# A graph layer with experts on one core: bucket ranks, counts and the last mixing moved to TensorE, slots spread out, short products put into waits

## The reference

```python
edge_index = jnp.stack([src, dst])                       # 100000 edges, 6250 nodes
xn = _layernorm(x)                                       # x: 6250 x 256
messages = xn[dst] * edge_weight[:, None]
agg = segment_sum(messages, src, 6250)
gin = relu((xn + agg) @ W1 + b1) @ W2 + b2               # 256 -> 512 -> 256
# mix: 8 heads; k, v = normed heads of xn; out = q (k^T v / N) + xn
x = x + gin + mix(xn)
y = _layernorm(x)
logits = y @ gate_w + gate_b                             # 16 experts, the best 2
h = relu(y @ w1[e] + b1[e]); o = h @ w2[e] + b2[e]       # 256 -> 512 -> 256
z = y + sum_k softmax(top2)[k] * o[k]
return x + layernorm(z) * gamma + beta
```

## Time and profile before

| what | value |
|---|---|
| median of 3 runs (lowest, highest) | 2381.49 us (2380.33, 2381.5) |
| profiled execution: its time, its span | 2381.34 us, 2379.1 us |
| block 1 | 0 to 501 us; counts ready at 92.5, sorting groups from 213 |
| block 2 | 501 to 1719.5 us; gathers issued 512.0 to 1687 |
| blocks 3 and 4 | 1719.5 to 2265.6 us; first expert tile's matmul 1753.69 |
| block 5 | 2265.6 to 2379.1 us |
| busy | PE 69%, DVE 61%, POOL 58%, ACT 31% |

### The profile page before, as it was taken

How to read it: one execution, slowest core, us unless ns; L and a number is a source line. 1 busy time by engine, 2 the same in 40 slices (tenths; PEclk the granted TensorE clock), 3 DMA queues, 4 the chain that set the end, 5 groups by cost and what they waited for, 6 DMA issues and landing times. The chain is left out here.

```text
span 2379.1 us, 40341 instructions
## 1 busy us (share of the span) xinstructions
PE 1638.3 (69%) x9284; PEld 1371.2 (58%) x9285; DVE 1453.1 (61%) x4177; ACT 739.9 (31%) x2173; POOL 1391.3 (58%) x1512
## 2 busy tenths in 40 slices
PE   5602788624556887787878777776569999999900
PEld 2202777613555776676766656654468888888800
DVE  8499988637676666666665665654343443434379
ACT  4803789500000344322222222221213333333200
POOL 8001788748876776677777777776225554555400
PEclk9856899856778999898898889888679999999955
DMA  4000011254333444344444444447581111111184
GB/s 153 0 0 16 20 35 34 20 104 134 115 113 89 133 127 120 108 128 120 127 121 125 124 119 125 124 118 98 77 288 57 62 62 57 60 61 61 52 290 149
DMA packets 133498, 233.44 MB, mean 98 GB/s; under 512 B 28775, under 2 KB 85199, under 8 KB 133374
## 3 DMA queue, kind: packets, MB, share of 16 engines
q0 software_dynamic: 56384, 145.17, 22.8%
q1 hardware_dynamic: 49294, 61.00, 8.4%
q10 hardware_dynamic: 27696, 25.83, 3.4%
HBM read 189.48 MB, written 42.43 MB: 97 GB/s over the span
## 5 line engine op out<-in xcount | busy, mean ns | idle before, releaser
L1278 POOL DMA_INDIRECT lower<-xn_rows,lower x864 | 865.0, 1001 | 310.5 <-issue 239.3
L1303 PE MATMUL bank<-lower 128*128 x960 | 342.9, 443 | 145.4 <-SPq L1154 121.3
L1439 DVE TENSOR_TENSOR xh<-xh,bank 128x256 f32 x480 | 199.7, 416 | 285.9 <-PE bank L1304 285.1
L1422 DVE TENSOR_SCALAR lower<-iota_n,lower 128x128 f32<-128x128 f32 x960 | 294.4, 357 | 69.7 <-issue 56.2
L606 POOL DMA_INDIRECT edge_records_sorted<-lower x112 | 200.8, 1793 | 205.1 <-ACT lower L717 174.9
L1304 PE MATMUL bank<-lower 128*128 x960 | 320.5, 419 | 0.0
L1303 PEld LDWEIGHTS bank<-lower 128*128 128x128 f32 x960 | 177.7, 213 | 212.1 <-issue 200.0
L650 PE MATMUL bank<-lower 128*64 128x128 f32 x1568 | 189.8, 285 | 125.1 <-ACT lower L701 120.8
L650 PEld LDWEIGHTS bank<-lower 128*64 128x64 f32 x1568 | 183.6, 145 | 128.8 <-DVE lower L915 121.4
L1834 POOL DMA_INDIRECT expert_rows<-arena,dest_idx x114 | 114.6, 1005 | 213.7 <-DVE arena L1929 196.5
L1920 DVE TENSOR_SCALAR arena<-bank,b_tile 128x128 f32<-128x128 f32 x456 | 128.4, 344 | 178.4 <-PE bank L1863 178.4
(11 more groups left out here) (316 smaller groups left out, 2530.4 us busy)
## 6 DMA issues: line engine op xcount, KB each, us to landing
lower<-xn_rows,lower POOLq DMA_INDIRECT x864
lower<-in_L_ffn_w SPq DMA_DIRECT2D x16, 512.0 KB, 9.7
upper<-in_L_ffn_w SPq DMA_DIRECT2D x16, 512.0 KB, 10.5
xn_rows<-xh SPq DMA_DIRECT2D x7, 896.0 KB, 4.1
arena<-xn_rows ACTq DMA_DIRECT2D x7, 896.0 KB, 5.5
lower<-xn_rows ACTq DMA_DIRECT2D x49, 128.0 KB
xn_rows<-lower ACTq DMA_DIRECT2D x49, 128.0 KB
x_plus_beta<-lower ACTq DMA_DIRECT2D x49, 128.0 KB
```

Source lines behind the costliest of these rows:

```text
L1278: pool.indirect_dma_start(edge_rows[:, t % ROUND, :], None, xn_dram, bass.IndirectOffsetOnAxis(source.bitcast(U32)[:, t:t + 1], 0)).then_i ...
L1303: pe.matmul(sums_at(u), edge_sel[:, 2 * u % ESEL, :], rows_flat[:, ds(at, D)], start=True, stop=False)
L1422: dve.tensor_scalar(edge_sel[:, (2 * u + h) % ESEL, :], iota_n[:], lane[:, at:at + 1], weight_s[:, at:at + 1], ALU.is_equal, ALU.mult).the ...
L1439: dve.tensor_tensor(xh[:, at], xh[:, at], sums_at(u), ALU.add).then_inc(s_acc, 1)
```

## The change

- **Counts and ranks.** Buckets are also stored place by place (`bkt_c`: for each of the 28 places the 28 groups side by side). Differences for a distance d are now two matmuls with the identity and its negative (`ident_b`, `minus_b`) into two banks, ScalarE squares from there and compares in bf16, and TensorE adds the result into banks 6 and 7 with the identity; GpSimd has no part. After every fourth distance TensorE does one counting round. Masks follow `bkt_c`, so a counting matmul reads runs of 28 neighbours. The two restart masks come from GpSimd, beside. The loop over buckets is written out and takes starts directly.
- **Fewer tiles.** ET is rounded up to 2 instead of 24: 858 tiles and 429 pairs (864 and 432 before); 480 units as before. The zeroed area stays at 864.
- **Order in block 2.** Slots are spread by 15/2 units instead of 14/3; `head_sums` eight units after a group's start; head rows are normed in place in two buffers, the next group loaded earlier; `stage_h` two units ahead; `mark` later, the last one in block 3.
- **Short products** (`spin`): ident x before, 128 columns fp32, into an unused part of bank 7: 38 in the last slot and its ranks, 18 at block 3, 25 at block 4.
- **Weights.** Block 3 loads only expert 0; experts 1 to 3 follow after the second row load of block 4 has landed. gamma is loaded in block 3.
- **Last mix.** ScalarE puts the mixing weights on diagonals, TensorE adds xh and both expert rows in a bank, VectorE reads mean, variance and values from it. The first and last groups are small (1, 1, 2, 3 and 3, 2, 1, 1 tiles), four row loads are in flight instead of three.

```diff
-    ET = -(-(NGRP * ((GC * P + NT * (QE - 1)) // QE)) // (TQ * ROUND)) * ROUND
+    ET = -(-(NGRP * ((GC * P + NT * (QE - 1)) // QE)) // (2 * TQ)) * 2
+    ZT = -(-ET // 8) * 8
@@ block 1, TensorE
+                def differences(d):
+                    if d > 2:
+                        pe.wait_ge(s_gapsq, d - 2)
+                    for h, lo, hi in halves_from(d):
+                        to = bank[2 + 2 * (d % 2) + h][:, 0:hi - lo]
+                        pe.matmul(to, ident_b, bkt_c[:, lo:hi], start=True, stop=False)
+                        mm = pe.matmul(to, minus_b, bkt_c[:, lo - d * NGRP:hi - d * NGRP], start=False, stop=True)
+                    mm.then_inc(s_gap, 1)
+                def add_same(d):
+                    pe.wait_ge(s_same, d)
+                    for h, lo, hi in halves_from(d):
+                        mm = pe.matmul(bank[6 + h][:, lo - h * EH:hi - h * EH], ident_b, same[d % 2][:, lo:hi],
+                                       start=False, stop=hi - lo == NGRP)
+                    mm.then_inc(s_local, 1)
-                    matched = match[p].rearrange("p (b g j) -> p b g j", g=NGRP, j=GC)
+                    matched = match[p].rearrange("p (b j g) -> p b j g", g=NGRP, j=GC)
-                        mm = pe.matmul(bank[p][:, 0:GT * NGRP], upto_b, matched[:, :, :, c], start=c == 0, stop=c == GC - 1)
+                        mm = pe.matmul(bank[p][:, 0:GT * NGRP], upto_b, matched[:, :, c, :], start=c == 0, stop=c == GC - 1)
+                for d in range(1, GC):
+                    add_same(d)
+                    if d + 2 < GC:
+                        differences(d + 2)
+                    if d % 4 == 3:
+                        count(d // 4)
@@ block 2
-        turn_unit = [max(slots_from + 1 + -(-14 * s // 3), done_by[s + 1] + 2) for s in range(NT)]
+        turn_unit = [max(slots_from + 1 + -(-15 * s // 2), done_by[s + 1] + 2) for s in range(NT)]
+        def spin(pe, n):
+            for _ in range(n):
+                pe.matmul(bank[7][:, D:D + P], ident[:], before[:], start=True, stop=True)
-                            if u == heads_from[g] + 4 + k // 2:
+                            if u == heads_from[g] + 8 + k // 2:
                                 head_sums(g, k)
+                        if u == rank_unit[-1]:
+                            spin(pe, 10)
+                    for f, later, spins in ((gate, T_GATE, 2), (turn_xn2, T_TURN2, 14), (second, T_SECOND, 6), (hidden, T_HIDDEN, 3),
+                                            (turn, 0, 3)):
@@ block 4, SP
+                    if e == 0:
+                        sp.wait_ge(s_tok[1], 16)
+                        for later in range(1, WAHEAD):
+                            load_weights(sp, later)
@@ block 5, TensorE
+                        if t >= FBANK:
+                            pe.wait_ge(s_fcen, t - FBANK + 1)
+                        pe.matmul(mixed, ident[:], xh[:, t * D:(t + 1) * D], start=True, stop=False)
+                        pe.wait_ge(s_fdiag, TOPK * (t + 1))
+                        pe.matmul(mixed, diag[t % NDG * TOPK], first_row(t), start=False, stop=False)
+                        pe.matmul(mixed, diag[t % NDG * TOPK + 1], second_row(t), start=False, stop=True).then_inc(s_fmix, 1)
@@ block 5, VectorE
-                        dve.scalar_tensor_tensor(first[k], first[k], weight(k, 0), xh[:, (t0 + k) * D:(t0 + k + 1) * D],
-                                                 ALU.mult, ALU.add).then_inc(s_dve, 1)
-                        dve.scalar_tensor_tensor(first[k], second[k], weight(k, 1),
-                                                 first[k], ALU.mult, ALU.add).then_inc(s_fmix, 1)
-                        dve.bn_stats(stats[:, k0 + k, :], first[k]).then_inc(s_dve, 1)
+                        dve.bn_stats(stats[:, k0 + k, :], bank[(t0 + k) % FBANK][:, 0:D]).then_inc(s_dve, 1)
```

More of the change, by code:

```diff
@@ L178, in gps_layer @@
         last_row = early(P)
-        apart = [early(EC) for _ in range(3)]
+        bkt_c = early(EC // 2).bitcast(BF16)
+        ident_b, minus_b = (early(P // 2).bitcast(BF16) for _ in range(2))
+        apart = [early(EC // 2).bitcast(BF16) for _ in range(2)]
+        same = [early(EC // 2).bitcast(BF16) for _ in range(2)]
         early = carver(row_hot[1], GC * P)
-        rank = early(EC)
-        same = [early(EC) for _ in range(3)]
+        restart_g, restart_b = (early(NT * NGRP) for _ in range(2))
         row_hot = [a.rearrange("p (j r) -> p j r", j=GC) for a in row_hot]
@@ L581, in _ @@
                                    pattern=[[0, P]], channel_multiplier=1).then_inc(s_consts, 1)
[L585 to L597, removed]
+                for a, first in ((restart_g, bg(restart_g)[:, :, 0:1]), (restart_b, gb(restart_b)[:, :, 0:1])):
+                    pool.memset(a, 1.0).then_inc(s_poolc, 1)
+                pool.wait_ge(s_poolc, 6)
+                for a, first in ((restart_g, bg(restart_g)[:, :, 0:1]), (restart_b, gb(restart_b)[:, :, 0:1])):
+                    pool.memset(first, 0.0).then_inc(s_restart, 1)
                 def scatter(r, i):
@@ L617, in _, with halves_from @@
             def _(pe):
[L619 to L622 removed]
+                pe.wait_ge(s_bkt, 2)
+                pe.wait_ge(s_upto, 3)
+                def halves_from(d):
+                    return [(h, max(d * NGRP, h * EH), (h + 1) * EH) for h in range(2) if d * NGRP < (h + 1) * EH]
+                def differences(d):
[6 more added lines that the diff above has]
+                    mm.then_inc(s_gap, 1)
@@ L629, in count @@
                     mm.then_inc(s_counted, 1)
-                run_steps(pe, count, 0, NR - 1, 1, (NR - 1) // 2)
+                for h in range(2):
+                    cols = slice(h * EH, (h + 1) * EH)
+                    pe.matmul(bank[6 + h][:, 0:EH], ident_b, bkt_c[:, cols], start=True, stop=False)
+                    pe.matmul(bank[6 + h][:, 0:EH], minus_b, bkt_c[:, cols], start=False, stop=False)
+                differences(1)
+                differences(2)
+                for d in range(1, GC):
[4 more added lines that the diff above has]
+                        count(d // 4)
@@ L849, in _ @@
                 dve.wait_ge(s_dve, n.add(3))
[L852 to L862, removed]
-                            matched[k] = n.add()
-                        if k >= 1:
-                            dve.wait_ge(s_dve, copied[k - 2] if k >= 2 else matched[0])
-                            dve.sem_inc(s_apart, 1)
-                            dve.copy_predicated(bg2(pos), bg2(masks[(k - 1) % 4]),
-                                                starts[(k - 1) % 4].unsqueeze(2).to_broadcast([P, NGRP, GC])).then_inc(s_dve, 1)
-                            copied[k - 1] = n.add()
-                    dve.wait_ge(s_dve, n.back(0))
-                    n.leave(NR)
@@ L1245, in _ @@
                 load(0)
-                with act.Fori(0, NG - 1) as g:
+                for g in range(NG):
                     heads(g)
-                heads(NG - 1)
                 act.wait_ge(s_kv, DC)
```

250 lines of the change are left out of this document (154 added, 96 removed).

## The result

The changed kernel takes **2254.34 us** (median of 4 runs, 2252.93 to 2255.62) against 2380.91 before (4 runs, 2374.72 to 2381.5): ratio **0.9474**, 95% interval 0.9457 to 0.9491. The forecast was 2258 (2242 to 2292). Its profiled execution took 2255.62 us, its span is 2253.7.

| stretch | before | changed | gained | forecast |
|---|---|---|---|---|
| start to last count copy | 92.20 | 54.27 | 37.9 | 37 |
| to the first sorting group | 120.8 | 106.8 | 14.0 | 11 |
| to the first gather | 299.0 | 296.0 | 3.1 | 0 |
| first to last gather issued | 1174.2 | 1119.7 | 54.5 | 39 |
| to the last unit's sum | 12.2 | 18.2 | -6.0 | 0 |

A forecast was written before the change was run, and what follows sets the result against it. No engine is full over the whole span, so each stage has its own limit. Gains of 37 + 11 + 29 + 10 + 6 + 31 = 124 us from 2381.5 give 2258 us, range 2242 to 2292 (own range 2244 to 2274).

The forecast's parts named there:

- 1, counts and ranks: Counting stage: joining counts and ranks on TensorE ends it at 55 us against 92.2, 37 us gained.
- 2, single instructions: Behind the counts on VectorE: masks moved, copy of starts dropped, bucket loop unrolled; net 11 us gained.
- 3, head sums and slots: Gathers: later head sums and wider slots remove waits for places; 29 us gained, bounds 0 and 34.2.
- 4, six loads less: Gathers: 858 loads instead of 864, 1.70 us each; 10 us gained, bounds 7.5 and 10.5.
- 5, the transition: Last gather to first expert tile: later marks, short products, later weights; sum -6 us, bounds +8 and -12.
- 6, last mix: Last stage: mixing on TensorE takes 82 us against 113.5, 31 us gained; bounds 36 and 22.
- the 87: Last stage in us if VectorE pays 62 cycles more per PSUM operation, 1.40 us a tile; not used in the sum.
- The early chain: Rival, counting stage: the run of 28 costs as the stride does, part 1 loses 12; 2307 us, chance 0.07.
- the kept waits of the gathers: Rival, gathers: spreading slots only moves the load, so waits stay; 2287 us, chance 0.14.
- the cold last stage: Rival, last mix: waiting for rows keeps TensorE at 0.50, the stage takes 143 us; 2319 us, chance 0.05.
- the slower rival: Rival, gathers: TensorE's in-order queue makes a unit dearer than GpSimd's pace; 2424 us at 2.9 a unit, chance 0.02.
- The products don't help: Rival, transition: short products fill no wait that costs, +8 instead of -6; 2272 us, chance 0.06.

The follow-up runs named there:

- e7: Changed kernel with masks group by group again, so counting matmuls read every 28th element; 2535.5 us on a chip with slower gathers.
- e12: Changed kernel with slots every 14/3 units and head sums four units after a group's start, both as before; 2299.77 us.
- e6: Changed kernel with 864 loads instead of 858, six more empty ones; 2482.44 us on a chip with slower gathers.
- e10: Changed kernel with weights of experts 0 to 3 loaded in block 3 and empty records naming different rows; 2233.13 us.
- e2: Changed kernel with experts 0 to 3 loading their weights in block 3; 2482.21 us on a chip with slower gathers.
- e1: Changed kernel without any of the 81 short products; 2487.23 us on a chip with slower gathers.
- e8: Changed kernel whose last mix loads only one of a node's two expert rows; last expert matmul to end 90.6 us, against 91.2.

## Why the prediction was right, point by point

- **What bounds each stage** was read rightly in three stages, block 1's two and the last mix, and these give 81 of the 125 us. In these stages a term is the time of the limiting engine.
- **1, counts and ranks: 37, measured 37.9.** The disputed price was the one of the run of 28: 0.084 us a matmul, 0.086 taken; 0.335 with the step (e7). The Trainium skill, SBUF — State Buffer, § Door 1: The DMA port swizzle, states lines of 16 bytes and a penalty for each access that crosses to a new one. The two prices, a factor of four, agree with that in kind; only these two steps were run, so the width of a line isn't shown. Off in the detail: ScalarE was not nearly full but 29.23 of 40.5 us, TensorE 33.24; the two hand work back and forth, and the allowances for that were about right.
- **2, single instructions: 11, measured 14.0.** The loop gained 9.3 (70.3 to 61.0, taken 8.7), masks 3.1, the rank add cost 0.7 (taken 0.8). Missing from the sum: the prefix sums on TensorE, whose result is read 5.39 instead of 7.39 us behind the last copy. They start as soon behind it (0.5 us) in both, but the first two rows of products took 1.92 and 1.79 us before and take 1.04 and 0.96 now, though the granted clock reads 1.00 in both; why is open.
- **3, head sums and slots: 29, under-sized.** All 34.2 us of waits ahead of the empty loads went, as the upper bound said; the discount of 5 was not needed. Undoing both parts costs even 47.6 (e12): in the new order they make 45.8 us of real waits ahead of the tail, 11.6 more than in the old one. Which of the other moves makes that was not tried, nor how the term splits between slots and head sums on this chip.
- **4, six loads less: 10, right at the issue and half given back.** Six steps of 1.25 and 3.3 us less waits in the tail are 10.8. But the last unit came 18.2 us behind the last issue instead of 12.2. 1.1 of these 6 us are the landing; 5.0 are sums. The prediction noted that the units stay 480 and put that at nothing: the three units that had pairs of their own now hang on the last pair, one behind the other. e6, with 864 loads, has the short end again. What bounds the tail itself e10 names: with other rows for the same descriptors 18.1 us go.
- **Not forecast at all:** a gather's issue takes 0.946 instead of 0.953 us and the step shrinks with it, 858 x 0.007 = 6 us (an estimate from the medians of the two profiles). e6 with 864 loads shows 0.946 too, so it is not their number; the cause stays open.
- **5, the transition: gain of 6, measured loss of 7.1. This is the term that failed**, in three places. (a) "+1.5" for 15 MB instead of 12 over the next tiles: it cost 7.2, and moving the weights back returned 6.5 (e2) and 5.4 (e10). The estimate took the extra bytes as spread; in fact TensorE waits for rows four times in these 50 us, 11.9 us in all against 5.5 before, and after the longest wait (4.21) it is cold. (b) "-3.4" for warm matmuls and "+1" for their time: the last slot's first layer stayed cold in this profile, the second had been warm before the change as well, and the 25 products of block 4 held up rows that had landed; by e1 the net worth lies between nothing and 5 us. (c) The marks moved later: ScalarE's six instructions for the slot before the last now stand ahead of the copy that starts the last slot, at 1597.56 instead of 1595.35, 2.2 us; the same engine order as before had that copy 0.1 us behind the sum. The 2.5 saved at the barrier (3.04 to 0.55) are mostly used up by that. This is read from the two timelines; no run has the marks back in their place.
- **6, last mix: 31, measured 29.1.** 84.4 us against 82; TensorE 59.57 of 60 busy at full clock, transfers no bound (e8). By the stage's time alone the 87 that the prediction worked out from the Trainium skill, VectorE: DVE Perf Modes, § The TRN2 errata, is as near as its 82. The rows decide: statistics from the bank take 0.425 us, 0.411 to 0.412 from SBUF before, 14 ns more, not the 65 (an estimate from the page's figure) that the 87 was worked out from; and VectorE is 53.16 of 60 us busy, so it isn't the bound. The 4 us for transfers were wrong in kind; the end was under-sized, 12.0 us behind TensorE's last product instead of 7.2.
- **Rivals.** The early chain, the kept waits of the gathers, the cold last stage and the slower rival did not come. "The products don't help" named +8 for the transition, and 7.1 were lost; but the weights lost them, and the products themselves are open between 0 and 5 us of gain.

## What to carry to other kernels

Follow a shortened queue to the last result that needs it: here half of what six loads less gained at the issue came back as sums on the last pair. Padding that points at one address is not free; spread it. Work that keeps an engine warm has to end before its real input lands, and a load moved out of one wait lies over the next one.

## What the runs showed of the hardware

- 128 descriptors that read the same 1 KB row: 1.64 to 1.70 us a load, DMA engines 0.89 to 0.96 busy for 85 or 86 GB/s; the same loads from different rows: 1.25 us, 0.40 busy, 120 GB/s (e10).
- Chips differ: the same kernel's gathers of random rows take 1119 us on one and about 1340 on two others, with 103 or 104 instead of 129 GB/s between 1000 and 1300 us, while the stages behind it agree within a few us. A gain in that stage has to be measured on the chip that it is meant for.
- A counting matmul with 196 columns of bf16 costs 0.335 to 0.337 us when it reads every 28th element, at a granted clock of 1.00 (before) and of 0.50 (e7) alike, and 0.084 us when it reads runs of 28 at 1.00.
- Short products on TensorE don't make its clock certain: the same matmuls behind the same products took 1.95 to 3.62 us in twelve profiled runs.
